# Adding x to chunk 0's product by accumulating loads, with chunk 0's second layer norm one phase later and the late weights in pieces

## The reference, cut to what matters

```
h    = rmsnorm(layernorm(x)) * gamma
q, kv, a = split(h @ w_qkva.T)            # 1024 -> 3 * 1024
a    = sigmoid(a);  y_t = a_t * y_(t-1) + kv_t
x    = x + q * y
z    = layernorm(x)
gate = softmax(z @ Wg + bg)               # 8 experts
out  = x + sum_e gate_e * (relu(z @ W1_e + b1_e) @ W2_e + b2_e)
```

## Time and profile before

| | |
|---|---|
| time of 3 runs, us | 328.88 median, 328.02 to 329.33 |
| the profiled execution | 328.83 us, span 327.3 us on core 4 |
| spans of the 8 cores | 325.3 to 327.3 us |
| PE busy | 314.1 us, 96% of the span |
| DVE, ACT, POOL busy | 186.2, 95.3, 59.1 us |
| A(0), A(1), F(0), core 4 | begin at 20.9, 70.9 and 118.1 us |
| A(2), core 4 | begins at 147.5 us |

### The profile page before, as it was taken

One profiled execution on the slowest core, in us unless ns is written; L12 is line 12 of the kernel. 1 busy time (PEld: TensorE's weight loads), 2 busy tenths in 40 slices (PEclk: granted clock), 3 DMA queues, 4 the chain that ended last, 5 costly groups with the idle time before them and its releaser, 6 DMA issues.

```text
span 327.3 us, 4910 instructions; the slowest of 8 cores (325.3 to 327.3 us)
## 1 busy us (share of the span) xinstructions
PE 314.1 (96%) x1570; PEld 142.4 (44%) x1601; DVE 186.2 (57%) x413; ACT 95.3 (29%) x148; POOL 59.1 (18%) x120
## 2 busy tenths in 40 slices
PE   7779998999999999999999999999999999999996
PEld 2335444454444444444444444444444434444442
DVE  0735478454778884453678774362678346734333
ACT  2382232663234323203325413103225520200000
POOL 4690003301311123001131313001131310000000
PEclk9999999999999999999999999999999999999999
DMA  5999999999991300866900300966000400154033
GB/s 93 252 147 171 194 228 206 222 178 225 195 216 34 132 0 6 162 222 223 250 39 0 132 0 16 180 222 228 2 0 1 131 0 0 43 173 175 0 125 132
DMA packets 18953, 40.53 MB, mean 124 GB/s; under 512 B 10128, under 2 KB 10416, under 8 KB 17904
## 3 DMA queue, kind: packets, MB, share of 16 engines
q1 hardware_dynamic: 15632, 25.47, 26.3%
q0 software_dynamic: 3296, 14.75, 24.4%
HBM read 40.25 MB, written 8.42 MB: 149 GB/s over the span
## 4 chain that ended last, share of the span: by engine, by line
PE 80%; DMA 14%; DVE 2%; POOL 2%; issue 1%; SPq 0%; DVEq 0%; POOLq 0%
PE ps L612 41%; PE ps L681 17%; PE ps L699 16%; DMA w<-xt 11%; DMA xtok<-xt 3%; PE ps L674 2%; PE ps L405 1%; PE ps L583 1%; POOL wq L531 1%; PE ps L310 1%; POOL wq L528 1%; PE ps L419 1%; DVE pb L337 0%; POOL w L231 0%; DVE xb L702 0%
## 5 line engine op out<-in xcount | busy, mean ns | idle before, releaser
L612 PE MATMUL ps<-pb,wq 128*128 128x512 bf16 x749 | 168.4, 379 | 3.2 <-DVE ry L279 1.4
L612 PEld LDWEIGHTS ps<-pb,wq 128*128 128x128 bf16 x768 | 74.4, 98 | 90.0 <-issue 5.3
L648 POOL TENSOR_TENSOR xb<-xb,sc 128x512 f32<-128x512 f32 x24 | 30.4, 1267 | 156.8 <-DVE sc L634 117.4
L681 PE MATMUL ps<-pb,w 128*128 128x512 bf16 x251 | 56.7, 379 | 0.3
L699 PE MATMUL ps<-h1g,w 128*128 128x512 bf16 x250 | 56.3, 379 | 0.4 <-issue 0.2
L619 ACT ACTIVATE asig<-ps 128x512 f32<-128x512 f32 x32 | 19.1, 596 | 109.8 <-PE ps L612 92.3
L625 DVE TENSOR_TENSOR_SCAN sc<-asig,carry,ps 128x512 f32<-128x512 f32 x24 | 30.7, 1279 | 32.0 <-PE ps L612 16.9
L702 DVE TENSOR_TENSOR xb<-ps,xb 128x512 f32<-128x512 f32 x32 | 22.1, 692 | 30.5 <-PE ps L699 30.5
L681 PEld LDWEIGHTS ps<-pb,w 128*128 128x128 bf16 x256 | 24.4, 98 | 30.1 <-issue 2.2
L699 PEld LDWEIGHTS ps<-h1g,w 128*128 128x128 bf16 x256 | 24.4, 98 | 29.9 <-issue 1.8
L684 DVE SCALAR_TENSOR_TENSOR h1g<-ps,grep 128x512 bf16<-128x512 f32 x32 | 22.1, 692 | 26.0 <-PE ps L681 25.9
(11 more groups left out here) (107 smaller groups left out, 168.3 us busy)
## 6 DMA issues: line engine op xcount, KB each, us to landing
xtok<-xt SPq DMA_DIRECT2D x12, 512.0 KB, 11.2
outd<-xb SPq DMA_DIRECT2D x12, 512.0 KB, 3.3
wq<-wqd POOLq DMA_DIRECT2D x7, 768.0 KB, 25.1
grep<-gscr SPq DMA_DIRECT2D x4, 1024.0 KB, 5.7
xb<-xd SPq DMA_DIRECT2D x8, 512.0 KB, 4.8
w<-xt POOLq DMA_DIRECT2D x4, 512.0 KB, 30.8
xb<-xd POOLq DMA_DIRECT2D x4, 512.0 KB, 51.7
w<-w1d POOLq DMA_DIRECT2D x2, 1024.0 KB, 57.7
```

What stands on the lines that cost most here:

```text
L612: mm[i] = PE.do(lambda e, k=k: e.matmul(ps[banks[i]][:], wq[:, j, i, k, :], hbc[:, k, :], start=(k == 0), stop=(k == KC - 1)), h[k] if j = ...
L648: x2 = POOL.do(lambda e: e.tensor_tensor(xc[:, j, :], xc[:, j, :], sc[s][:], ALU.add), at, x_t[c][j])
L681: t = PE.do(lambda e, k=k: e.matmul(ps[b][:], w1[:, e_, k, :], xbf_of[c][:, k, :], start=False, stop=(k == KC - 1)), C[c]["xbf"][k] if e_ ...
```

## The change

- Chunk 0's product `at` is written straight into `xb[0]`, and x is added to it by four DMAs of POOL's queue that accumulate into SBUF (`add_xd`, two groups each). The 32 transposes, the 8 adds on DVE and the fourth bank go. The first three are put at the hook (6, 2) of A(0), the fourth after A(0).
- All of chunk 0's `cs_step` and its 16 row matmuls move into A(1).
- The five small constants and the identity come in one load, between chunk 0's second and third load of x; b1's four loads come after the head.
- `wq` of groups 5, 6 and 7 comes in three loads each, one for each projection.
- On POOL's queue w1, b2 and the last half of chunk 1's x move behind the accumulating loads, after A(0)'s POOL work. Chunk 2's token-major x is loaded after A(1)'s first x2.
- `w1_sums` becomes `w1_parts`, 16 matmuls of 128x32 by 128x512 in four column groups of the array, with an evacuation in two bfloat16 parts, and a second step of 2 matmuls for each half. `w1_parts` does both halves at the hook (5, 0) of A(1).
- Chunk 2's `ln1_bn` moves from A(1) to the first four experts of F(0), and its seed, norm, transposes and gamma four places on or, for gamma, one.

```diff
+        def add_xd(q):
+
+            t = POOL.dma(lambda e: e.dma_start(out=xb[0][:, 2 * q:2 * q + 2, :], in_=xd[0, :, q * 1024:(q + 1) * 1024],
+                                               accum_op=ALU.add), chan(f"d_xa{q}"), C[0]["at"][2 * q + 1])
+            C[0]["x2"][2 * q] = t
+            C[0]["x2"][2 * q + 1] = t
...
-            if j == 0:
+            if j == 0 or j > 4:
                 wq_t[j] = [POOL.dma(lambda e, i=i: e.dma_start(
-                    out=wq[:, 0, i], in_=wqd[0, :, i * 1024:(i + 1) * 1024]), chan(f"d_wq0{i}")) for i in range(3)]
+                    out=wq[:, j, i], in_=wqd[j, :, i * 1024:(i + 1) * 1024]), chan(f"d_wq{j}{i}")) for i in range(3)]
...
+        def w1_parts():
+            banks = [ring_take() for _ in range(2)]
+            for h in range(2):
+                b = banks[h]
+                for k in range(KC):
+                    g = k % 4
+                    t = PE.do(lambda e, k=k, g=g, h=h, b=b: e.matmul(
+                        ps[b][32 * g:32 * g + 32, :], selw[:, 0:32], w1[:, 4 * h:4 * h + 4, k, :], start=(k < 4),
+                        stop=(k >= 4)),
+                        w1_t[h], ms["selw"], ring_free[b] if k == 0 else None, tick=(k == KC - 1))
+                hi = ACT.do(lambda e, h=h, b=b: e.activation(w1p[h][0], ps[b][:], AF.Copy), t, *xn_free)
+                w1part[h] = DVE.do(lambda e, h=h, b=b: e.tensor_tensor(w1p[h][1], ps[b][:], w1p[h][0], ALU.subtract),
+                                   hi)
+                ring_free[b] = w1part[h]
...
-            for k in range(KC):
-                t = PE.do(lambda e, k=k: e.matmul(ps[b][:], selw[:], w1[:, 4 * h:4 * h + 4, k, :], start=(k == 0),
-                                                  stop=(k == KC - 1)),
+            for k in range(2):
+                t = PE.do(lambda e, k=k: e.matmul(ps[b][:], fold[:].rearrange("p r m -> p (r m)"), w1p[h][k],
+                                                  start=(k == 0), stop=(k == 1)),
...
+                dst = xc[:, j, :] if c == 0 else sc[s][:]
+                at = DVE.do(lambda e: e.tensor_tensor(dst, ps[bq][:], sc[s][:], ALU.mult), mm[2], cy)
                 if c == 0:
-                    bx = ring_take()
-                    for i in range(NT):
-                        tx = PE.do(lambda e, i=i: e.matmul(
-                            ps[bx][:, i * 128:(i + 1) * 128], xtok[:, i, j * 128:(j + 1) * 128], ident[:],
-                            start=True, stop=True, is_transpose=True),
-                            xt_t[0][i], id_t, ring_free[bx] if i == 0 else None, tick=(i == NT - 1))
-                    x2 = DVE.do(lambda e: e.tensor_tensor(xc[:, j, :], ps[bx][:], sc[s][:], ALU.add), tx, at)
...
+        add(hk, (6, 2), lambda: (add_xd(0), add_xd(1), add_xd(2)))
         phase_a(0, hk)
+        add_xd(3)
+        load_xd(1, 2, lane=POOL)
+        load_xd(1, 3, lane=POOL)
+        load_w1(0)
+        load_w1(1)
+        load_b2()
         load_w2()
...
+        for k, p in enumerate([(0, 2), (0, 2), (1, 1), (1, 1), (1, 2), (2, 1), (2, 1), (2, 2)]):
+            add(hk, p, lambda k=k: cs_step(0, k))
+        add(hk, (3, 0), lambda: (rows_step(0, KC - 1, KC), rows_out(0)))
+        add(hk, (3, 1), lambda: fwd_transposes(0))
+        slices(hk, lambda: ln2_small(C[0]["fwd"]), [(3, 1), (3, 2), (3, 2), (4, 0), (4, 2), (5, 0)])
+        add(hk, (1, 2), lambda: [load_xt(2, i, C[1]["x2"][0]) for i in range(NT)])
+        add(hk, (5, 0), w1_parts)
+        add(hk, (6, 0), lambda: w1_sums(0))
+        add(hk, (6, 1), lambda: w1_sums(1))
...
+            o = 4 if c == 2 else 0
+            if c == 2:
+                bn_hooks(hooks, c, [("h", n) for n in range(NT)])
+            at = lambda n: ("h", n) if n < E else ("y", n - E)
+            add(hooks, at(o), lambda: ln1_seed(c, 0, NT))
+            add(hooks, at(o), lambda: ln1_small(c, 0, NT))
             for n in range(NT):
-                add(hooks, ("h", 4 + n // 2), lambda n=n: ln1_norm(c, n))
-                add(hooks, ("h", 7), lambda n=n: ln1_turn_dma(c, n))
+                add(hooks, at(o + 4 + n // 2), lambda n=n: ln1_norm(c, n))
+                add(hooks, at(o + 7), lambda n=n: ln1_turn_dma(c, n))
             for k in range(KC):
-                add(hooks, ("y", 4 + k // 4), lambda k=k: ln1_gamma(c, k))
+                add(hooks, ("y", 4 + k // 4 + o // 4), lambda k=k: ln1_gamma(c, k))
```

More of the change, by code:

```diff
@@ L119, in build_program @@
         ones = sb("ones", [128, 128], BF16)
-        ident = sb("ident", [128, 128], F32)
+        fold = sb("fold", [128, 4, 32], BF16)
+        cst = sb("cst", [128, 273], F32)
+        ident = cst[:, 0:128]
+        wgf = cst[:, 128:256].rearrange("p (a b) -> p a b", b=16)
+        gam = cst[:, 256:264]
+        bgr = cst[:, 264:272]
+        nm = cst[:, 272:273]
         identb = sb("identb", [128, 128], BF16)
[L122 to L125, removed]
         wgs = sb("wgs", [128, E], F32)
@@ L191, in build_program, with load_x0 @@
         ms["junk"] = DVE.do(lambda e: e.memset(grep[:, 0, :], 0.0))
-        id_t = SP.dma(lambda e: e.dma_start(out=ident[:], in_=idd), chan("d_id"))
         xt_ch = [chan(f"d_xt{i}") for i in range(NT)]
         xt_t = {0: []}
-        for i in range(NT):
-            xt_t[0].append(SP.dma(lambda e, i=i: e.dma_start(
+        def load_x0(i):
+            xt_t[0].append(SP.dma(lambda e: e.dma_start(
                 out=xtok[:, i, :], in_=xt[0, :, i * D:(i + 1) * D]), xt_ch[i]))
[L198 to L204, removed]
+        load_x0(0)
+        load_x0(1)
+        cst_t = SP.dma(lambda e: e.dma_start(out=cst[:], in_=cstd), chan("d_cst"))
+        id_t = gam_t = wgf_t = bg_t = nm_t = cst_t
+        load_x0(2)
+        load_x0(3)
         ring = {"i": 0}
@@ L520, in build_program @@
         st["psT"], psR_free[0], psR_free[1], ring_free[4] = [C[0]["h"][k] for k in (2, 3, 6, 7)]
+        b1_ch = chan("d_b1")
+        SP.wait(C[0]["xn"][NT - 1])
+        for r in range(4):
+            b1_t = SP.dma(lambda e, r=r: e.dma_start(out=b1f[32 * r + 16:32 * r + 24, :], in_=b1d), b1_ch, ms["b1"])
         POOL.wait(xt_t[0][1])
@@ L555, in load_w2, with load_b2 @@
                     C[1]["xn"][NT - 1]))
-        load_w1(0)
-        load_xd(1, 2, lane=POOL)
-        load_w1(1)
-        load_xd(1, 3, lane=POOL)
         b2_ch = chan("d_b2")
-        for r in range(4):
-            b2_t = POOL.dma(lambda e, r=r: e.dma_start(out=b2p[32 * r:32 * r + E, :], in_=b2d), b2_ch, ms["b2"])
+        b2_t = []
+        def load_b2():
+            for r in range(4):
+                t = POOL.dma(lambda e, r=r: e.dma_start(out=b2p[32 * r:32 * r + E, :], in_=b2d), b2_ch, ms["b2"])
+            b2_t.append(t)
         wgs_tok = None
@@ L766, in build_program @@
             add(hk, p, lambda kp=kp: ln1_turn(1, kp, dve=(kp % 2 == 1)))
-        stat_hooks(hk, 0)
         gate = {}
         for lo, p in ((0, ((4, 0), (4, 1), (5, 1))), (2, ((5, 0), (5, 1), (6, 1)))):
-            add(hk, p[0], lambda lo=lo: (ln1_bn(1, lo), ln1_bn(1, lo + 1)))
+            add(hk, p[0], lambda lo=lo: ln1_bn(1, lo))
+            add(hk, p[0] if lo == 0 else p[1], lambda lo=lo: ln1_bn(1, lo + 1))
             add(hk, p[1], lambda lo=lo: (ln1_seed(1, lo, lo + 2), ln1_small(1, lo, lo + 2)))
@@ L782, in bn_hooks @@
                 add(hooks, p, lambda n=n: ln1_bn(c, n))
         hk = {}
-        ln2_hooks(hk, 0, A_PLACES)
+        for k, p in enumerate([(0, 2), (0, 2), (1, 1), (1, 1), (1, 2), (2, 1), (2, 1), (2, 2)]):
[3 more added lines that the diff above has]
+        slices(hk, lambda: ln2_small(C[0]["fwd"]), [(3, 1), (3, 2), (3, 2), (4, 0), (4, 2), (5, 0)])
+        add(hk, (5, 2), lambda: back(0))
```

80 lines of the change are left out of this document (40 added, 40 removed).

## The result

| | before | after |
|---|---|---|
| median of 4 runs, us | 328.91 | 333.66 |
| the profiled execution | 328.83, span 327.3 on core 4 | 333.95, span 332.4 on core 0 |
| ratio, 95% interval | | 1.0143 [1.0121, 1.0164] |

Slower by 1.4%. Of the four runs after, one (361.02 us) had a die at a lower clock; such runs count in the medians given in this text, but not in the ratios and their intervals, and differences between kernels are read from the ratios. The forecast was 333.4 us. It came out right as a total; of its two big terms one was 3.7 us too high and the other 3.7 too low.

A forecast was written before the change was run, and what follows sets the result against it. It took PE's work as the bound from A(1) on and POOL's DMA queue in A(0). Span 327.3 plus 0.9 at F(0) and 3.7 at A(2) gave 331.9, with 1.5 around it 333.4 us; range 326.8 to 342.

The forecast's parts named there:

- its two big terms: F(0) starting 0.9 us later after a wait for w1, and A(2) 3.7 us more from chunk 2's late transposes.
- Head and A(0): Start to A(1): head 0.3 us sooner, group 6 at 54.8, A(1) at 67.1 instead of 70.9.
- PE stands at its second half until 103.5: At `w1_parts` in A(1): PE waits about 5.8 us for w1's second half, F(0) starting at 118.95.
- An accumulate: 2.55 us taken: On POOL's queue: each 512 KB accumulating load priced like w2's written bytes, 2.55 us, bounds 1.45 and 5.1.
- W1's sums: End of A(1): PE's work on the sums falls from 3.56 to 1.1 + 0.87 us, 1.6 saved.
- The transposes: SP's queue, F(0) to A(2): start at F(0) + 23.7, land at 31.6, delay PE 3.7 us, bounds 2.7 and 5.2.
- the clock as what could add to the time: Whole kernel: PE's waits might make the granted clock fall, adding time; no size given.
- The sum: Core 4's span: 327.3 plus 0.9 at F(0) and 3.7 at A(2), 331.9; with 1.5 around it 333.4 us.
- w1 comes in time: Rival at A(1): w1's second half lands by 97.2, F(0) starts 4.85 us earlier, 327.7 us; chance 22%.
- Accumulates at twice the price: Rival on POOL's queue: 5.1 us per accumulate, w1's second half at 113.7, F(0) 11.1 later, 343.6 us; chance 20%.
- the transposes are hidden: Rival at F(0) to A(2): SP gets past its store sooner, w1 still waits, 329.7 us; chance 8%.

The follow-up runs named there:

- experiment 9: The kernel with both repairs (norms and transposes before stores, ACT's order turned), accumulating loads undone, chunk 0's x on PE transposes again; 327.12 us, ratio 0.9954 to before.
- experiment 6: The changed kernel with chunk 2's token-major x loaded from the end of A(0), as before the change; 335.62 us, ratio 1.0207 to before.
- experiment 5: The changed kernel with b2's four small loads put behind w2 on POOL's queue; 335.77 us, a single run.
- experiment 4: The changed kernel with the four accumulating loads made plain loads of the same bytes; 335.11 us, ratio 1.0192 to before.
- Experiment 7: The changed kernel with chunk 2's norm where it was and chunk 1's fourth `cs_step` ahead of chunk 0's exponential on ACT; 326.55 us, ratio 0.9929 to before.
- experiment 10: The kernel before the change with only W1's sums by columns alone (`w1_parts` at (5, 0)); 327.55 us, ratio 0.9970 to before.
- Experiment 2: The changed kernel with chunk 2's transposes ahead of the first store, alone (328.59 us) or with all four norms at (y, 0) too (327.08 us).
- the second form of experiment 2: The changed kernel with chunk 2's four norms and four transposes at (y, 0), ahead of the first store; 327.08 us, ratio 0.9958 to before.
- experiments 8: The changed kernel with chunk 2's norms and transposes ahead of the first store and chunk 1's fourth `cs_step` before the exponential; 327.10 us, ratio 0.9945 to before.
- experiment 3: The changed kernel with 20 unused matmuls at the start of A(2) to keep PE busy; 333.96 us, ratio 1.0157 to before.
- experiment 1: The changed kernel with chunk 2's statistics, seed, norm, transposes and gammas back at their old places; 328.38 us, ratio 0.9985 to before.
- its copy: The changed kernel, unedited, run again on the second chip; 335.34 us, ratio 1.0186 to before.

## Why the prediction came out right, point by point

**Head and A(0): right on the slow cores.** A(1) was forecast at 67.1 and starts at 67.12 on core 0. Group 6 was to come at 54.8 and comes at 53.35, after 1.44 us for the first third of its weights, 1.4 us earlier than forecast; what was missed, 0.92 us at chunk 1's turns for ACT's norms (`xn`), gives most of this back. From core 4 before to core 0 after the head brought 0.8 us instead of 0.3; core by core it is 0 to 1.3 us on the slow cores and 1.7 to 2.3 on the others. That the rest of PE's saving in A(0) goes to the queue is shown by experiment 9: the transposes' removal brings 0.7, and the other 2.1 of the 2.8 us between A(0)'s and A(1)'s start (49.8 before, 47.0 after) come with the edits beside it. Which of them (the row sums moved out, the weights in thirds, the loads moved back in the queue) was not taken apart.

**The step that failed: "PE stands at its second half until 103.5".** The mechanism, w1 at the end of a longer queue, is there, but w1's second half landed at 96.5 and is in time; F(0) came at 115.2 instead of 118.95. Of these 7 us of landing, experiment 6 shows about 2: chunk 2's x no longer competes with w1, but only begins at 75 us. I had counted it as present in both. b2, 1.3 us at most, went the same way (experiment 5; it lay ahead of w2, whose landing was my yardstick, and lies behind w1 now). Part of the rest is that the queue ran ahead: chunk 1's last x tile landed at 79.8 us where the forecast has 81.9. The second had landed at 62.8 instead of 66.6, and part of that lead went in waiting for the accumulates to be issued. Some 2 us stay open.

**An accumulate: 2.55 us taken, 2.5 measured** in a full queue (experiment 4). The four landed at 66.7, 69.6, 72.1 and 75.9 us; the mean distance of 3.1 has in it the fourth, which is issued 5.2 us after the third and lands in among the x tiles behind it. The rule of the Trainium skill, page "Collectives: The Full Stack", section "The bandwidth ceiling: the fold count and why AG ≠ RS ≠ AR", would have it at twice a copy, and the trace agrees: 2.5 us against 1.25 for a plain load of x, 178 GB/s against 416. What the prediction had wrong beside it was the price of the copy. It set 2.58 us, the mean of all traffic, where a plain load takes half of that, and so the 5.1 us of its rival is twice a load with a cast, not twice a copy.

**Missed in A(1): ACT.** The row sums for chunk 1 wait 1.39 us, 1.9 with what is lost around it, for a cast behind the late exponential. Together with the 0.55 of moved row sums this makes A(1) to W1's first sum 32.1 us instead of 29.7. Experiment 7 takes the wait away. The forecast followed the moved `ln2_small` only as far as the queue's landings, not into the order of ACT.

**W1's sums: right in the changed kernel** (16.0 us from first sum to F(0), 17.6 before: the 1.6 forecast), though experiment 10 shows that 1.0 is what they bring where DVE is less free.

**The transposes: right in place, sized too low.** Forecast: they start at F(0) + 23.7, the last goes at 27.9 and lands at 31.6, and delay PE 3.7. Measured: start at F(0) + 24.4, issue 6.92 instead of 5.4, and the stretch 7.4 us longer: 4.6 idle at A(2) (4.0 to 5.2 by core), 0.4 at F(0)'s second group of experts, where DVE with its statistics is late after all, 0.8 for late tiles in A(2)'s first group, and 1.5 for the granted clock. The forecast named the clock as what could add to the time, and put no price on it. Experiment 2 shows the cause: with the transposes in front of the stores all of it goes but the 0.4 to 0.5 us of DVE, at unchanged norms.

**The sum.** F(0) 2.8 us earlier instead of 0.9 later, A(2)'s row sums 7.4 later instead of 3.7. The errors of 3.7 cancel; the 333.4 is right by that luck, not by its working. Of the rivals, *w1 comes in time* is what happened; the price that I gave it, 327.7, assumed the same 3.7 at the transposes and no new wait, and with the measured 7.4 and the 1.9 on ACT it would have been 333.3. *Accumulates at twice the price*, 5.1 us each, and *the transposes are hidden* fell.

## What to carry to other kernels

A DMA issue that is moved to a later hook is priced by what stands in front of it on its queue there: here the place behind two stores that wait for their results and a load that waits for one of them cost 7.5 us, and the place in front of them nothing. When a landing is forecast by the volume of a queue, all queues that run beside it belong in the sum; 2 MB that begin later on SP's queue brought w1 2 us forward. And work that is taken off the busiest engine in a stretch already near the arrival of its loads (A(0)), or near DVE's limit (the end of A(1)), brings a fraction: 0.7 of 3.5 us and 1.0 of 1.6. When a rule speaks of a ratio, such as an add at half the rate of a copy, the copy's price is to be read from rows of that copy in a full queue, and not from a mean of other traffic.

The version to keep is experiment 7's: 326.55 us, 0.7% faster than before. It is the changed kernel with chunk 2's norm where it was and ACT's order at (5, 0) turned. The intervals of the second form of experiment 2 and of experiments 8 and 9, 0.4 to 0.6% faster, overlap with its, so that its place ahead of them isn't shown; and experiment 9, which keeps the transposes on PE, is as fast as 8.

## What the runs showed of the hardware

- **The clock after a short idle.** After 4.15 us without a matmul PE ran at a granted clock of 0.51 and 0.63 over the next two windows of 4 us (core 0), which cost about 1.5 us by experiment 3, as the mean of the cores.
- **A fall of a whole die to 0.81** for 7.5 to 9.5 us between 74 and 88 us, with PE fully busy, in the profiled executions of seven kernels: die 0 in the four of the first chip, die 1 in experiments 6, 8 and 9 on the third, and in experiment 6 also cores 0 and 1, for 15 us from 81 us on. Those of the first chip had an earlier one, 5 to 7 us from 28 to 30 us on (two cores of experiment 1 another at 46 us). There is none in those of before, after and its copy, nor in four others (all on the second chip among them). Where it comes between A(1) and W1's first sum for 7.5 to 9.5 us it costs 1.2 to 1.6 us. The Trainium skill, page "TensorE: Matmul & The Clock Gate", section "Part 1: The HAM clock gate (the "warmup" mystery)", has a limiter of peak current that takes a whole die to 13/16 while several of its cores run dense matmuls. The level, 0.81, and the four cores of a die agree; that it should last as long as the load doesn't, since the matmuls go on for 240 us. What sets it off here is open.
- **Issue costs on POOL.** An accumulating load occupied it 0.85 to 1.56 us, the same load without the add 0.53 to 0.61; w1's issues, 0.88 here, took 0.55 in experiment 4.
- **An accumulating load at half the rate of a plain one.** In a full queue 512 KB took 2.5 us with the add and 1.2 to 1.3 without (experiment 4).
- **The issue of DMA transposes** took 5.4 to 5.5 us for four on all cores of before and of experiment 1, 6.4 to 7.8 in the changed kernel, and 5.8 to 7.5 in experiment 2, where no store stands in front of them. What slows them isn't shown.
